# One block for routing, experts and combine, with the row gathers paced by TensorE, in a mixture-of-experts decoder layer

## The reference, cut to what matters

```python
x = _layernorm(x + _L0_attn_ref(x, Wq, bq, Wk, bk, Wv, bv))        # x: 128 x 64 x 128, so 8192 tokens of 128
x = _layernorm(x + _L0_xattn_ref(x, ctx_1024, ctx_1024))
x = _layernorm(x + _L0_ffn_ref(x, gate_W, w1_e, w3_e, w2_e, w1_s, w3_s, w2_s))

def _L0_ffn_ref(...):                                              # 8 experts, 2 per token, hidden size 512
    probs = softmax(flat @ gate_W.T)
    top_v, top_i = top_k(probs, 2)
    gates = zeros(T, 8).at[arange(T)[:, None], top_i].set(top_v)
    out_e = einsum('etf,efd->etd', silu(flat @ w1_e) * (flat @ w3_e), w2_e)
    routed = einsum('te,etd->td', gates, out_e)
    shared = sum over 8 slices of (silu(x @ w1_s) * (x @ w3_s)) @ w2_s / 8
    return 0.5 * shared + 0.5 * routed
```

## Time and profile before

| | us |
|---|---|
| three runs | 846.84, 850.24, 852.47 |
| median of them | 850.24 |
| the profiled execution, its own time | 843.65 |
| its span, first to last instruction | 841.9 |
| of it attention, up to the first shared-expert matmul of routing | 209.4 |
| routing, to the first expert matmul | 209.4 to 323.8 |
| experts, to the last `down` | 323.8 to 754.2 |
| combine | 754.2 to 841.9 |
| busy: PE, DVE, ACT, POOL | 713.6, 487.4, 481.5, 461.6 |

### The profile page before, as it was taken

How to read it: one execution, slowest core, us unless ns; L and a number is a source line. 1 busy time by engine, 2 the same in 40 slices (tenths; PEclk the granted TensorE clock), 3 DMA queues, 4 the chain that set the end, 5 groups by cost and what they waited for, 6 DMA issues and landing times.

```text
span 841.9 us, 16996 instructions
## 1 busy us (share of the span) xinstructions
PE 713.6 (85%) x5112; PEld 650.7 (77%) x5113; DVE 487.4 (58%) x1435; ACT 481.5 (57%) x1441; POOL 461.6 (55%) x471
## 2 busy tenths in 40 slices
PE   5789999874999996898888888989889888999950
PEld 3668888763788885898888888888889887898750
DVE  3798999864899753433434343334333434446896
ACT  5889999821399722544445344445444444544796
POOL 3378988852111155266766666666666666541322
PEclk9999999875999997899999999999999999999985
DMA  5457555523211232011111111111111112215573
GB/s 172 151 176 227 176 181 168 151 75 102 74 51 51 76 84 64 24 41 42 44 44 41 44 41 44 44 44 41 41 44 44 44 42 42 38 58 154 149 217 109
DMA packets 87238, 72.57 MB, mean 86 GB/s; under 512 B 10067, under 2 KB 72411, under 8 KB 87195
## 3 DMA queue, kind: packets, MB, share of 16 engines
q1 hardware_dynamic: 77808, 53.43, 21.5%
q0 software_dynamic: 9088, 18.63, 8.3%
q10 hardware_dynamic: 298, 0.01, 0.0%
HBM read 50.14 MB, written 21.89 MB: 86 GB/s over the span
## 4 chain that ended last, share of the span: by engine, by line
PE 46%; issue 7%; DVE 5%; ACT 2%; another core or an unknown queue 1%; DMA 1%; ACTq 0%; POOLq 0%; POOL 0%; SPq 0%; DVEq 0%
PE bank L1325 15%; PE bank L1293 9%; PE bank L1294 9%; PE bank L1295 9%; PE bank L1285 2%; DVE xg L1609 2%; DVE f_st L1626 1%; DVE z L1620 1%; DVE f_hT L1597 1%; ACT xg L1571 1%; DMA f_x2T<-x2T_cols 1%; PE bank L1513 0%; PE bank L1512 0%; PE bank L1511 0%
## 5 line engine op out<-in xcount | busy, mean ns | idle before, releaser
L1403 DVE TENSOR_TENSOR e_hT<-e_sg,bank 128x512 f32<-128x512 f32 x142 | 97.7, 688 | 258.5 <-PE bank L1295 109.4
L1266 POOL DMA_INDIRECT y_rows<-e_y,dst_tab x142 | 148.0, 1042 | 108.5 <-ACT e_y L1357 75.8
L1293 PE MATMUL bank<-e_x_hi,e_w_hi 128*128 128x256 f32 x568 | 179.0, 315 | 29.9 <-issue 27.0
L1294 PE MATMUL bank<-e_x_lo,e_w_hi 128*128 128x256 f32 x568 | 167.1, 294 | 8.6 <-issue 7.8
L1295 PE MATMUL bank<-e_x_hi,e_w_lo 128*128 128x256 f32 x568 | 166.9, 294 | 4.2 <-issue 4.0
L1258 POOL DMA_INDIRECT xg<-x_rows,src_tab x130 | 130.1, 1001 | 55.1 <-issue 36.0
L1351 ACT ACTIVATE e_sg<-bank 128x512 f32<-128x512 f32 x142 | 84.6, 596 | 116.7 <-PE bank L1295 76.0
L1325 PE MATMUL bank<-w,e_hT 128*128 x1136 | 142.7, 279 | 4.7 <-issue 4.4
L1293 PEld LDWEIGHTS bank<-e_x_hi,e_w_hi 128*128 128x128 f32 x568 | 114.0, 201 | 37.1 <-issue 32.7
L1325 PEld LDWEIGHTS bank<-w,e_hT 128*128 128x128 f32 x1136 | 136.5, 196 | 6.0 <-issue 5.7
L1295 PEld LDWEIGHTS bank<-e_x_hi,e_w_lo 128*128 128x128 f32 x568 | 114.3, 201 | 9.5 <-issue 9.2
(11 more groups left out here) (172 smaller groups left out, 1544.2 us busy)
## 6 DMA issues: line engine op xcount, KB each, us to landing
yk<-y_rows SPq DMA_DIRECT2D x16, 512.0 KB, 4.4
xT_in<-in_xT_dram SPq DMA_DIRECT2D x16, 256.0 KB, 3.3
x_res<-in_x_dram SPq DMA_DIRECT2D x16, 256.0 KB, 3.6
w_in<-in_L_ffn_w_e_dram SPq DMA_DIRECT2D x16, 256.0 KB, 3.0
c_in<-in_ctx_dram SPq DMA_DIRECT2D x16, 256.0 KB, 2.9
cT_in<-in_ctxT_dram SPq DMA_DIRECT2D x16, 256.0 KB, 3.2
x_rows<-x SPq DMA_DIRECT2D x16, 256.0 KB, 2.4
x2T_cols<-x2T SPq DMA_DIRECT2D x16, 256.0 KB, 2.7
```

The costliest lines, as they stand in the source:

```text
L1266: nc.gpsimd.indirect_dma_start(y_rows, bass.IndirectOffsetOnAxis(dst_tab[:, n:n + 1], 0), y[b % R][:, t, :], None).then_inc(scattered[b % ...
L1293: nc.tensor.matmul(at, w_hi[r % 2][:, w], x_hi[r][:, :], start=True, stop=False)
L1294: nc.tensor.matmul(at, w_hi[r % 2][:, w], x_lo[r][:, :], start=False, stop=False)
L1403: nc.vector.tensor_tensor(hT[par][:, half * HC:(half + 1) * HC, :].rearrange("p c n -> p (c n)"), sg[half][:, :], bank[2 + half][:, :], AL ...
```

## The change

Routing, experts and combine become one block: no barrier between routing and experts, and each engine's program runs routing, then experts, then combine. `LateRows` becomes `Common`, which holds the tiles that the three now share (x2T, x_hi, x_lo, sg, hT). Some things are done ahead, inside routing's last four steps: the first transposes of PE (steps 37 and 38; in step 39 PE waits for `w_at_ok`), the weights and x parts of blocks 0 and 1 on ACT and DVE (steps 36 to 39). The table is read back one step earlier and in two steps instead of four (steps 30 and 31), and `w_at` is made in steps 32 and 33.

The gathers: a ring of 16 blocks (XR) instead of 8 + 4. Of the 142 gathers, 16 are issued in routing's steps 32 to 39, each after PE's `g_ps` or `u_ps` of that step, 8 in expert steps 0 and 1, each after one of their four `g_ps` or `u_ps`, and 118 in the steps b = 0 to 61, 1.9 a step, after the two scatters of block b; the first waits for `u_ps` of the first half of PE's step b + 2, the second for `g_ps` and the third, if there is one, for `u_ps` of the second half. The last 9 steps have none.

The loop over blocks 8 to 67 is gone: all 71 blocks are written out on PE, ACT and DVE. LEAD in combine is 8 instead of 6.

```diff
-EARLY_X, RING, PRE = 8, 4, 6
+XR, RING = 16, 4
@@ routing
-    LOOK = C0 + NC + 1
+    LOOK = C0 + NC
-            pool.wait_ge(src_ok, 1)
-            for b in range(PRE):
-                for t in range(BT):
-                    n = b * BT + t
-                    nc.gpsimd.indirect_dma_start(xg[b][:, t, :], None, x2_rows,
-                                                 bass.IndirectOffsetOnAxis(src_tab[:, n:n + 1], 0)
-                                                 ).then_inc(gathered[b], 16)
+        pool.wait_ge(src_ok, 1)
...
+            ahead(n - EARLY * FC)
...
+    return Programs(sync=sync, gpsimd=gpsimd, tensor=tensor, scalar=scalar, vector=vector,
+                    ups=(g_ps, u_ps), table_at=LOOK + 2, rows_in=late_ld)
@@ experts
-        for b in range(LOOP[0] * R):
-            step(b, b // R, b % R)
-        with engine.Fori(*LOOP) as j:
-            for r in range(R):
-                step(j * R + r, j, r, inner=True)
-        for b in range(LOOP[1] * R, NB + 2):
+        for b in range(NB + 2):
             step(b, b // R, b % R)
...
-        for b in range(PRE, EARLY_X + R):
-            gather(b)
+        first = 2 * (EARLY * FC - m["zero"].table_at)
+        for i in range(first):
+            n = EARLY * FC - first // 2 + i // 2
+            pool.wait_ge(m["zero"].ups[i % 2], n + 1)
+            gather(i)
+        done = first
+        for n in range(2 * 2):
+            for ups in (g_ps, u_ps):
+                pool.wait_ge(ups, n + 1)
+                gather(done)
+                done += 1
+        ahead = done
         for b in range(NB):
             scatter(b)
-            if EARLY_X + R <= b + 2 * R < NB:
-                gather(b + 2 * R)
+            upto = min(NBT, ahead + -(-(NBT - ahead) * (b + 1) // (NB - 9)))
+            for i in range(done, upto):
+                pool.wait_ge((u_ps, g_ps, u_ps)[i - done], 2 * (b + 2) + (1, 2, 2)[i - done])
+                gather(i)
+            done = upto
...
-        for b in range(2):
-            transpose_x(b, 0, b)
+        def ahead(n):
+            if n == -1:
+                pe.wait_ge(late.w_at_ok, 1)
+            if -3 <= n < -1:
+                transpose_x(n + 3, n + 3)
@@ combine
-    LEAD = 6
+    LEAD = 8
...
+        dve.wait_ge(rows_in, 16 * LATE)
```

More of the change, by code:

```diff
@@ L199, in _ @@
                 def _(pe):
-                    one.tensor(pe)
+                    ahead, run = one.tensor(pe)
+                    zero.tensor(pe, ahead)
+                    run()
                     two.tensor(pe)
@@ new lines, in routing, with sb @@
+    common = m["common"]
+    def sb(name, shape, dt=F32):
+        return m["work"].enter_context(nc.sbuf_tensor(name, shape, dt))
+    NK = NT * K
+    OC, C0 = 6, 2 * FC
+    NC = -(-NK // OC)
+    LOOK = C0 + NC
+    assert LOOK + 6 <= EARLY * FC
+    pick = [sb(f"pick{k}", [P, NT, E]) for k in range(K)]
+    pos = [sb(f"pos{n}", [P, NT, E]) for n in range(2)]
+    upto = sb("upto", [P, NT, E])
+    both = sb("both", [P, NT, E], BF16)
+    slot = sb("slot", [P, NT, K])
+    slot_i = sb("slot_i", [P, NK], I32)
@@ new lines, in routing @@
+    end = sb("end", [P, E])
+    start = sb("start", [P, E])
+    blk = sb("blk", [P, NK], BF16)
+    row = sb("row", [P, NK], BF16)
+    code = sb("code", [P, NK])
+    own = [sb(f"own{n}", [P, NB]) for n in range(2)]
+    found, place, moved = (pick[0][:, :, :].rearrange("p t e -> p (t e)")[:, n * NBT:(n + 1) * NBT] for n in range(3))
+    found_i, at_i = (pick[1][:, :, :].rearrange("p t e -> p (t e)")[:, n * NBT:(n + 1) * NBT].bitcast(I32)
+                     for n in range(2))
+    at_t, at_p = (pos[1][:, :, :].rearrange("p t e -> p (t e)")[:, n * NBT:(n + 1) * NBT].bitcast(I32)
+                  for n in range(2))
@@ new lines, in scalar, with x_high, codes @@
+    def scalar(act, ahead):
+        act.wait_ge(exp_in, 1)
+        nc.scalar.activation(e8[:, :, :], e8[:, :, :], ACT.Exp).then_inc(exp_ok, 1)
+        def x_high(g):
+            act.wait_ge(x_ld, 16 * (g + 1))
+            nc.scalar.activation(x_hi[g % 2][:, :], x2T[:, :], ACT.Copy).then_inc(x_hi_ok, 1)
+        def codes(i):
+            act.wait_ge(oh_ok, i + 1)
+            if i >= 2:
+                act.wait_ge(oh_used, i - 1)
+            for q, n in enumerate(pairs(i)):
+                last = nc.scalar.activation(oh_code[i % 2][:, q, :], oh_blk[i % 2][:, q, :], ACT.Copy,
+                                            scale=code[:, n:n + 1])
+            last.then_inc(code_ok, 1)
+        x_high(0)
+        for n in range(EARLY * FC):
+            g, c = divmod(n, FC)
+            act.wait_ge(g_ps, n + 1)
+            if n >= 2:
+                act.wait_ge(hT_ok, n - 1)
+            nc.scalar.activation(sg[c % 2][:, :], bank[c % 2][:, :], ACT.Silu).then_inc(sg_ok, 1)
+            if c == 1 and g + 1 < EARLY:
+                x_high(g + 1)
+            if 0 <= n - C0 < NC:
+                codes(n - C0)
+            ahead(n - EARLY * FC)
@@ L1329, in step @@
                 last.then_inc(y_ps, 1)
-        steps(pe, step)
+        return ahead, lambda: steps(step)
     def scalar(act):
@@ L1463, in combine @@
     st = pair("f_st", [P, GT, 6])
-    sg = pair("f_sg", [P, GN])
-    hT = [[sb(f"f_hT{n}_{c}", [P, GN]) for c in range(FC)] for n in range(2)]
+    sg, hT = late.sg, late.hT
     y_ld = [sem(f"f_y_ld{n}") for n in range(R)]
```

662 lines of the change are left out of this document (309 added, 353 removed).

## The result

The changed kernel takes 838.55 us (median of 4 runs, 837.39 to 840.04), the kernel before 849.57 us beside it: a ratio of 0.9867 (95% interval 0.9838 to 0.9895). It is faster by 11 us, where 41 were forecast. The profiled execution took 838.74 us, its span is 836.6 us.

What follows compares the result with a forecast made beforehand. Late PE updates during POOL's unbroken indirect DMAs, with POOL near its rate limit, were taken to bound the expert blocks. Terms -8.7 - 10.5 + 4 - 29 + 2.9 = -41.3 gave 809 us for the median (802 profiled), range 771 to 851.

Steps and rivals of the forecast that it cites:

- The mechanism: Expert stage and bursts: POOL's unbroken runs of indirect DMAs hold back PE's updates, 3.5 to 5.1 us late, until POOL pauses.
- my own sign of a forecast wrong in its root: Updates late while POOL stands still, or on time through runs of eight and more, would show the forecast wrong.
- the silu at 336.11: Second burst, kernel before: came after 7.32 us of idling though its matmul ended at 330.97; read as a late PE update.
- the 118 gathers: Expert steps 0 to 61: paced gathers bring blocks from 6.17 to 5.6 us, between bounds 5.07 and 6.17; gain 29 us.
- Rival A: Expert blocks: the waits do little, only scatters pause POOL, blocks stay at 6.17 us; 844 us, chance 0.22.
- B: Rival, cured: late updates never reach PE's margin, POOL's rate is the bound, new bursts cost nothing; 772 us, chance 0.20.
- C: Rival, slower: waits hold POOL, which holds PE through the result ring; blocks 6.47 us, 871 us in all, chance 0.14.
- The 24 gathers: Routing's end and blocks 0 and 1: gathers replacing the old bursts, nearly as dense but each waiting for PE; cost 4 us.
- the term for the barrier and the preparation: Between routing and experts: late updates, barrier and first blocks' preparation go or move into routing steps 36 to 39; gain 8.7 us.
- The 10.5 for the second burst: From 323.84 to 345.42: 21.6 us where clean would be 11.1; 10.5 us go with the 12 gathers in a row.
- Written out: Expert loop: the jump back costs nothing and written-out code, though it has to be fetched, none either; 0 us.
- LEAD 8: Combine: two more PE steps put group 0's DVE work 4.6 us later, one dear group fewer saves 1.7; 2.9 us lost.

Runs made afterwards that it cites:

- before, last group: The unedited kernel before, run once for its trace in the last group of experiments: 849.75 us, interval 6.27.
- after, last group: The unedited changed kernel, run once beside the kernel before in the last group of experiments: 837.43 us, interval 6.03.
- without the waits: The changed kernel without its 142 waits for a later update of PE, where updates stick: 840.35 us, ratio 0.9973 to the kernel before.
- the kernel with waits and `memset`: The changed kernel with a memset of one column on POOL after each indirect DMA from the expert steps on: 830.91 us, one run.

## Why the prediction was wrong

**The mechanism held, on some occasions.** POOL's indirect DMAs hold back PE's updates: not POOL's being busy, not the traffic, not code. The dose, from all groups where updates stick: 1.9 or 2 a block, 4.88 us; 3, 4.90; 3.9, 6.03 to 6.09; 4, 6.16 and 6.27. But my own sign of a forecast wrong in its root, updates on time through runs of eight and more, did appear in two of five groups: there the same programs ran whole stretches of 186 unbroken DMAs with nothing late. What sets this wasn't found, and no run could choose it. The expectations speak of a chip where updates stick, but it isn't settled by the chip: the group at 778.01 us and, 21 minutes later, that at 846.65 us were both on chip 15. One reading of the prediction was off as well: the silu at 336.11 is the first of its block and took a product that ended at 329.32, so that update came 6.8 us late, not 5.1.

**The step that failed is the 118 gathers: "I take 5.6, the middle".** It put the gain at 29 us; the two pairs of traces have -1.3 and 8.7. The blocks took 6.09 us and 6.03 with the waits, 6.04 without. POOL's account shows where the time goes, from 376 to 620 us in five traces (pauses are gaps between two DMAs of over 0.5 us):

```
                         interval   pauses   in all, us   mean, us
before                       6.16       25         41.3       1.65
before, last group           6.27       29         43.1       1.48
after                        6.09       25         40.3       1.61
after, last group            6.03       37         42.4       1.15
without the waits            6.04       20         41.5       2.08
```

The waits make pauses more and shorter, and leave their sum where it was: 40.3 us in some 40 blocks, 1.0 us a block. Added to POOL's own 3.9 x 1.3 = 5.07 us that is the 6.09. This sum proves nothing by itself: a block's time is always POOL's work plus its pauses, so where the interval stays the same, the sum must too. What the traces add is how far into a pause the first held update lands. Between POOL's last DMA record and the first update of PE that lands in the pause, there is a median of 1.0 us in the profile after, 0.7 in the last group's and 1.16 without the waits, far more than the 0.3 us between two DMAs of a run. In the prediction's words POOL, "the busier of the two, loses the time that it stands"; I gave that half its weight. So a wait moves the pause, but the pause that frees an update is still paid. With three indirect DMAs and a plain one POOL has 3 x 1.3 + 0.6 = 4.5 us of work in the 4.88, and its pauses mostly come out of what is left. That the pauses are needed in this sum, and aren't just what happens, is my reading; no run set pauses of a chosen length.

**Where they stand doesn't matter.** Rival A said that only scatters would pause POOL. In the profile after they do for 35.1 of 56.6 us; in the last group's run of it, gathers do for most (34.6 us from 376 to 620, remote and PE, against 13.2 at scatters). The time is the same, 838.55 and 837.43 us. A's 844 is the nearest figure, its reason half right. B (772) has the bound right for the occasions where nothing sticks (5.1 us of POOL's work a block), but not for this one. C fell: a block took 6.09 and 6.03 us, not 6.47.

**The 24 gathers: 4 us were taken, about 9.6 measured.** Routing's last `down` ended at 322.3 instead of the 315.2 that 4.7 us of work give (7.1 us), and the two first blocks took 15.4 us from 322.3 to 337.7, where 2 x 1.79 + 3 x 3.09 = 12.9 would do (2.5 us). With nothing stuck the first expert matmul came at 313.3, with a burst that began 1.6 us earlier: 314.9 in this trace's time, where the prediction put 315.1. So the term for the barrier and the preparation (8.7) is borne out where nothing sticks, and what was priced too low is the replacement of the old bursts. The 10.5 for the second burst is a reading of the trace before. The prediction trusted that "each waits for an update younger than the one before it waited for". POOL reached the first one late, and twelve found their updates waiting.

**What the waits are worth is here.** Without them y1 ends at 346.9, with them at 337.7 and 338.0: 9 us. That is also the difference of the ratios, 0.9973 without and 0.9867 with, which are 1.06% of 845 us apart. These come from different groups, between which the kernel before spreads from 842 to 850 us; but within one group the kernel with waits and `memset` took 830.91 us and that without waits 840.35, 9.4 us apart. So nearly all that the change gains over the kernel before hangs on the waits of the first 24 gathers, and in the blocks the waits are worth nothing that shows.

**Written out: 0, as taken.** 4.88 us a block in all clean stretches. The Trainium skill (Runtime: NRT & Kernel Launch, Instruction fetch mechanics) has taken branches to code outside the window as a reason to unroll; neither the jump in the earlier trace rows nor its removal shows a microsecond of it. That is no test of the rule, since no instruction packet moved between 400 and 520 us. In the profile after, the packets of the instruction queue q8 rose from 19 to 40, and no clean block is longer for it.

**LEAD 8: combine is 2.9 us longer, as forecast, and 2.6 in the other pair.** But undoing LEAD alone gave back only 1.5 us of combine, and 0.8 us of the total, too little to be told from nothing. So LEAD is shown for half of the term; that the whole came out at 2.9 is in part luck, and what the rest is stays open.

**What stays open.** Where nothing sticks the change gains 16.5 us (777.2 to 760.69), more than where updates stick, and the waits have no part in it (760.83 without). How that splits between the start and the blocks can't be said: there is no trace of the kernel before from such a group. No edit made a version that beats the changed kernel and still computes the whole: LEAD 6 is within the interval, and the `memset` has the changed kernel's ratio, from one run. Whether what counts is the number of indirect DMAs in a row or their share of POOL's time was not separated: with three a block a plain DMA broke the runs, and the share of the stretch fell too, from 67% to 64%.

## What to carry to other kernels

Before pacing an engine's queue, ask whether that engine is the bound: if it is, a wait that binds takes its time from the bound, and what helped here was fewer of its instructions (one indirect DMA less a block out of four, if the kernel can spare it). A wait for an update that is already there when the queue comes to it does nothing; look at when the queue arrives, not at when the update is due. And spread prefetches only as far as the stock lasts when the issuing engine never catches up: four steps more cost 18.5 us where nothing sticks.

## What the runs showed of the hardware that was not expected

The kernel before took 842 to 850 us in three of the five groups (and beside the result), and 777 and 778 us in the other two; the changed one 837.43 and 838.55 us, or 760.69. Of the 80.3 us between the spans of the changed kernel's traces (836.6 and 756.3), 11.3 lie before y1, 68.9 in the blocks and 0.1 in combine. The clock isn't it: in the stretch from 376 us it was granted at 0.98 in the one and 1.00 in the other, while a block takes 6.09 us and 4.98. In the one kind most of PE's updates come late while POOL issues indirect DMAs (185 of 235, half of these by over 2 us), in the other none of 294 does. Both kinds occurred on chip 15, 21 minutes apart. So a time of this kernel means something only beside another of the same group.

An indirect DMA of 128 rows costs POOL 0.94 to 1.06 us on average and 0.30 us of issue, a plain one of the same bytes 0.58 us. The Trainium skill (Perfetto Trace Analysis, DMA Instruction — SWDGE (GPSIMD)) says that the end which the profiler reports for such a DMA is that of the making of its descriptors, not of the transfer; the trace agrees, since PE waited for the rows until 651.90 with POOL's record of the last gather before it, at 649.49, over at 650.52.
